# Three-layer graph block: each engine's order within a turn rewritten, the layer boundary made chunk by chunk, tables loaded in three parts

## The chip, the cores and the metric

The kernel runs on one core of one Trainium2 chip. The metric is device time in microseconds (us) of one execution; the median of three runs of the kernel before is 1787.18 us. The engines: PE (TensorE, matmuls and transposes), DVE (VectorE), ACT (ScalarE), POOL (GpSimd, which here issues the indirect DMAs and multiplies one tile), SP (SyncE, which issues the plain DMAs).

## The reference

10,000 nodes with 512 features, 5,000 edges sorted by destination. First a three-layer graph network with batch norm:

```
x_l: h = x @ W[l].T ; agg = segment_sum(h[src] * norm, dst) + b[l]      (every node also has a loop edge)
     x = relu(gamma[l] * (agg - mean) * rsqrt(var + 1e-5) + beta[l])     (mean, var over all nodes)
```

`x` plus its result goes through a layer norm. Then an equivariant message layer over the same edges and another layer norm give the output. The change touches the three layers alone.

## The kernel before

Four stages follow each other: `order_edges` sorts edges and loads tables; `graph_layers` computes the three layers; `finish_gcn` adds and norms; `messages` and `touched` do the rest. All the edits but the first (the table loads at the end of `order_edges`) are in `graph_layers`.

Nodes are held in 20 blocks of four tiles a layer, features on the partitions, in four chunks `c` of 128 features. `kinds` names the blocks P P E P E P ... E P E E: an E (edge) block has 4 x 127 nodes that are destinations of edges, a P (plain) block 4 x 123 nodes that are not. In an E block the sums over the edges are made first ("merge") and added to the block's own rows ("join").

Each engine's program is a list of turns t; in turn t block t is multiplied and the blocks ahead are prepared. There is no planner: the order is written out by hand in each engine's `body(layer, t)`, and semaphores order the engines. In a turn, j counts the four output chunks or the four tiles of a block:

- PE: `products(t, j)`, 12 matmuls of 492 or 508 columns (high and low parts of both factors, three products for each of four chunks; each first waits for `lo` of its chunk); `back(t-1, j)`, four transposes that give node rows for the next layer's table (layers 0 and 1 only); `turn_in(t+2, j)`, four transposes of gathered rows (layer 0 only); `merge(t+2, j)`, four matmuls with the edge table (E blocks).
- ACT: `copy` of a product out of PSUM into `aggT` (L891), `high` (L844, L846), `relu` of the block loaded from `z` (L860), `sources`, relu of gathered rows (L867), `rows_out` copies of `back` (L899), `plain` (L853).
- DVE: `low` (L757, L759), `bn_stats` of a copied chunk (L796), merge with the running carry (L737, L739), `join` (L750), `shifts` of gathered rows (L768), `build` of the edge tables (layer 0).
- POOL: indirect DMAs: `own` (L646: node rows into R, layer 0), `gather` (L631: edge source rows), `place` (L636: node ids of E blocks), `leave` (L652: result rows into the next layer's table), the scatter of payload (L676, layer 1); and in layers 1 and 2 one multiply of an E block by its own weights (L670).
- SP: loads of `z`, stores of `aggT` to `z`, stores of R (L608).

Rings: R has 8 buffers, G 4 (8 with R's first four in layers 1 and 2), X 3, yhi, ylo, aggT and every PSUM tile 2, V 4. In layer 0 the ids of E block b are fetched in turn b-5 and used in turn b-3.

At a layer's end turn NB does the last `back`s, `rows_out` copies and scatters. Then DVE makes the batch-norm factors of all four chunks at once (`factors`, L702 to L710) and ACT the root (L916), which stands behind the last `rows_out` copy in ACT's order; only then does ACT take relu and high of the next layer's first blocks.

## Time and profile before

| | us |
|---|---|
| median of three runs | 1787.18 (1779.79 to 1788.62) |
| the profiled execution | 1788.72 |
| its span | 1786.9 |
| PE busy | 1383.3 (77%) |
| DVE busy | 1219.7 (68%) |
| POOL busy | 965.3 (54%) |
| ACT busy | 946.7 (53%) |
| granted clock of PE, mean | 0.868 of full speed |

The stages in time: ordering to 170 us; layer 0's products from 200.5 to 536, layer 1's from 554.5 to 855, layer 2's from 868 to 1181; the rest to 1787. Busy shares are averages over stages with different limits, so what a stage is bound by is read from its own windows and waits. Busy time of a matmul counts its whole passage, so neighbours overlap: what a matmul costs in a row of them is the distance from one start to the next.

### The profile page before, as it was taken

What the parts mean: (1) busy time and instruction counts of PE and PEld (TensorE: products, weight loads), DVE (VectorE), ACT (ScalarE), POOL (GpSimd) and SP (SyncE); (2) the same over time, 40 slices, a digit from 0 to 9 for tenths busy, and PEclk for the clock granted to TensorE, in tenths of its full rate; (3) what the DMA queues carried; (4) which work ended last, traced back from release to release, by engine and by line L of the source; (5) the groups of instructions that cost most, each with busy time, mean ns of one, the idle gap of its engine ahead of it and who ended that gap; (6) DMA issues with size and microseconds to landing.
All of it is one profiled execution on the core that took longest, in us unless ns stands there. A gap on an engine that the chain in (4) does not pass through costs nothing. (4 is left out here: it accounts for less than half of the span.)

```text
span 1786.9 us, 27336 instructions
## 1 busy us (share of the span) xinstructions
PE 1383.3 (77%) x8020; PEld 1181.3 (66%) x8020; DVE 1219.7 (68%) x3372; ACT 946.7 (53%) x1900; POOL 965.3 (54%) x966
## 2 busy tenths in 40 slices
PE   4574699999995999999698988863555269999733
PEld 3454588888784888888576777753444158888622
DVE  6357467666565676767577768857777459999765
ACT  3471244353335767674555554436778624444476
POOL 4770777777744677777523223204777744343146
PEclk8797799999998999999899999976655679999955
DMA  2002878888775677776644545359999433333112
GB/s 60 2 2 82 263 244 282 274 274 272 261 266 198 216 258 239 252 253 208 219 135 157 171 161 168 113 196 298 412 401 404 201 101 85 92 89 87 42 69 111
DMA packets 130634, 340.36 MB, mean 190 GB/s; under 512 B 34940, under 2 KB 67188, under 8 KB 127702
## 3 DMA queue, kind: packets, MB, share of 16 engines
q1 hardware_dynamic: 74198, 175.45, 28.0%
q0 software_dynamic: 56320, 163.51, 27.4%
q8 instruction: 55, 0.90, 0.2%
q14 instruction: 61, 0.50, 0.1%
HBM read 166.40 MB, written 177.40 MB: 192 GB/s over the span
## 5 line engine op out<-in xcount | busy, mean ns | idle before, releaser
L946 PE MATMUL ps_b<-yhi,whi 128*128 128x492 f32 (+1 forms) x960 | 399.4, 416 | 33.9 <-DVE ylo L759 25.2
L946 PE MATMUL ps_b<-ylo,whi 128*128 128x492 f32 (+1 forms) x960 | 380.2, 396 | 0.0
L946 PE MATMUL ps_b<-yhi,wlo 128*128 128x492 f32 (+1 forms) x960 | 379.9, 396 | 0.0
L891 ACT COPY aggT<-ps_b 128x492 f32<-128x492 f32 (+1 forms) x240 | 137.4, 573 | 307.1 <-PE ps_b L946 306.8
L796 DVE BATCH_NORM_STATS2 stat<-aggT 128x6 f32<-128x492 f32 (+1 forms) x240 | 162.3, 677 | 155.4 <-ACT aggT L891 155.4
L652 POOL DMA_INDIRECT rows<-rows_out,node_at x160 | 175.1, 1095 | 123.7 <-ACT rows_out L899 84.6
L946 PEld LDWEIGHTS ps_b<-yhi,whi 128*128 128x128 f32 x960 | 186.9, 195 | 67.5 <-issue 26.2
L946 PEld LDWEIGHTS ps_b<-yhi,wlo 128*128 128x128 f32 x960 | 185.1, 193 | 38.5
L946 PEld LDWEIGHTS ps_b<-ylo,whi 128*128 128x128 f32 x960 | 186.4, 194 | 30.4 <-issue 0.5
L759 DVE SCALAR_TENSOR_TENSOR ylo<-X,bn_scale,yhi 128x492 fp32r<-128x492 f32 (+1 forms) x160 | 147.3, 962 | 78.0 <-ACT yhi L846 78.0
L670 POOL TENSOR_TENSOR X<-X,own_row 128x2032 f32<-128x2032 f32 x20 | 91.6, 4579 | 176.1 <-ACT X L860 176.0
L1173 PE MATMUL fin_ps_x<-ident,fin_X 128*123 128x128 f32 (+1 forms) x320 | 72.1, 396 | 99.1 <-DVE fin_xr L1098 73.0
L1173 PEld LDWEIGHTS fin_ps_x<-ident,fin_X 128*123 128x123 f32 (+1 forms) x320 | 63.9, 292 | 115.0 <-DVE fin_xr L1098 77.4
L737 DVE SCALAR_TENSOR_TENSOR V<-cont,carry,ps_m 128x127 f32<-128x127 bf16 x480 | 132.4, 339 | 3.6 <-PE ps_m L933 2.3
L646 POOL DMA_INDIRECT R<-in_x,node_at x80 | 93.4, 1167 | 71.1 <-DVE rows_out L813 47.0
L1047 POOL DMA_INDIRECT x<-fin_x,node_at x80 | 78.8, 985 | 94.7 <-ACT fin_x L1150 74.6
L846 ACT ACTIVATE yhi<-X,bn_scale 128x492 fp32r<-128x492 f32 (+1 forms) x160 | 104.9, 705 | 23.3 <-DVE X L750 23.2
L899 ACT COPY rows_out<-ps_c 123x512 f32<-123x512 f32 (+1 forms) x160 | 94.6, 592 | 33.8 <-DMA rows<-rows_out,node_at 32.4
L933 PE MATMUL ps_m<-sel,G 128*128 128x128 f32 x640 | 89.8, 286 | 23.0 <-DVE carry L739 14.4
L957 PEld LDWEIGHTS ps_c<-ident,aggT 128*127 128x127 f32 (+1 forms) x640 | 94.0, 187 | 14.1 <-ACT aggT L891 0.8
L860 ACT ACTIVATE X<-X,bn_shift 128x492 f32<-128x492 f32 (+1 forms) x160 | 100.4, 702 | 1.6 <-DVE bn_scale L708 1.6
L933 PEld LDWEIGHTS ps_m<-sel,G 128*128 128x128 f32 x640 | 81.6, 199 | 29.2 <-issue 17.0
(346 smaller groups left out, 3196.5 us busy)
## 6 DMA issues: line engine op xcount, KB each, us to landing
z<-aggT SPq DMA_DIRECT2D x30, 1016.0 KB, 4.8
z<-aggT SPq DMA_DIRECT2D x30, 984.0 KB, 6.0
x_rows<-R SPq DMA_DIRECT2D x80, 256.0 KB, 4.3
fin_xr<-x_rows SPq DMA_DIRECT2D x20, 1024.0 KB, 8.3
X<-z SPq DMA_DIRECT2D x20, 1016.0 KB, 7.5
X<-z SPq DMA_DIRECT2D x20, 984.0 KB, 7.6
fin_X<-z SPq DMA_DIRECT2D x10, 1016.0 KB, 12.5
fin_X<-z SPq DMA_DIRECT2D x10, 984.0 KB, 13.5
```

Of the source, the lines that this page charges most:

```text
L652: pool.indirect_dma_start(table[layer], bass.IndirectOffsetOnAxis(ap=k.node_at[:, i:i + 1], axis=0), f.rows[j][:], None, bounds_check=m.N ...
L737: nc.vector.scalar_tensor_tensor(V3[i % 4][:, c, :], k.cont[:, i, 0:EPT], f.carry[i % 2][:, c:c + 1], ps[:, c, 0:EPT], ALU.mult, ALU.add)
L759: nc.vector.scalar_tensor_tensor(f.ylo[g % 2][:, c, 0:n], y, s.scale[:, c:c + 1], hi, ALU.mult, ALU.subtract).then_inc(x["lo"], 1)
L796: nc.vector.bn_stats(k.stat[:, j, 6 * t:6 * t + 6], f.aggT[t % 2][:, j, 0:n]).then_inc(x["counted"], 1)
L846: nc.scalar.activation(f.yhi[g % 2][:, c, 0:n], f.X[g % 3][:, c, 0:n], ACT.Copy, scale=s.scale[:, c:c + 1]).then_inc(x["hi"], 1)
L860: nc.scalar.activation(f.X[g % 3][:, c, 0:n], f.X[g % 3][:, c, 0:n], ACT.Relu, bias=s.shift[:, c:c + 1]).then_inc(x["act_x"], 1)
L891: nc.scalar.copy(f.aggT[t % 2][:, j, 0:cols(t)], f.ps_b[j % 2][:, 0:cols(t)]).then_inc(x["copied"], 1)
L899: nc.scalar.copy(f.rows[j][0:n, :], f.ps_c[j % 2][0:n, :]).then_inc(x["rows"], 1)
L933: o = nc.tensor.matmul(f.ps_m[i % 2][:, c * P:(c + 1) * P], buffer[:, c * P:(c + 1) * P], k.sel[:, i * P:(i + 1) * P], start=True, stop=True)
L946: o = nc.tensor.matmul(f.ps_b[j % 2][:, 0:n], w[:, c, j * P:(j + 1) * P], y[g % 2][:, c, 0:n], start=(c == 0 and i == 0), stop=(c == C - 1 ...
L957: o = nc.tensor.transpose(f.ps_c[j % 2][0:n, c * P:(c + 1) * P], f.aggT[b % 2][:, c, col:col + n], k.ident[:])
L1173: o = nc.tensor.transpose(k.ps_x[j % 2][0:n, c * P:(c + 1) * P], f.X[b % 3][:, c, col:col + n], k.ident[:])
```

## The change

In words, by engine:

- `order_edges` loads only the first of now three parts of the match and own tables (tiles 0 to 4; before 0 to 7 and 8 to 39, both here). SP loads parts 1 (5 to 16) and 2 (17 to 39) in turns -1 and 0 of layer 0.
- POOL: the first gathers each wait for the memset of their own buffer, not for all twelve; ids of E block b are fetched in turn b-4; the multiply is made in two halves of two chunks; the payload scatters go four to each plain turn; turn NB is gone, its scatters come after the last turn.
- DVE: `join` works by chunk over all four tiles of a block and not by tile over all four chunks; lows of a plain block all come at the top of the turn; `shift` is spread over j; the first E block of layers 1 and 2 is merged and joined in turn 1.
- ACT: highs of a plain block at the top of the turn, two relus before and two after copy 0; `source` spread over j; its own order for turn 0 of layers 1 and 2.
- The boundary: in the last turn of a layer each chunk's aggregate, root and factors follow its statistics, and relu, high and low of that chunk of the next layer's block 0 follow at once; the last block's `back`s and `rows_out` copies stand partly before and partly behind the next layer's first product.

```diff
@@ order_edges, SP
-            for i, (lo, hi) in enumerate(k.parts):
-                sp.dma_start(k.sel[...], a.match_rows[...]...).then_inc(k.match_in[i], 16)
-                sp.dma_start(own[...], a.own_rows[...]...).then_inc(k.own_in[i], 16)
+            lo, hi = k.parts[0]
+            sp.dma_start(k.sel[...], a.match_rows[...]...).then_inc(k.match_in[0], 16)
+            sp.dma_start(own[...], a.own_rows[...]...).then_inc(k.own_in[0], 16)
@@ graph_layers
     def each_turn(body, layer):
-        for t in range(-5, NB + 1):
+        for t in range(-5, NB):
             body(layer, t)
+    def ends(layer, t):
+        return t == NB - 1 and layer < L - 1
@@ SP, after the four R stores of a turn
+                if layer == 0 and 0 <= t + 1 < len(k.parts) - 1:
+                    tables(t + 2)
@@ POOL
             def own(b, j):
...
+                if n < 8:
+                    pool.wait_ge(x["zero"], n + 1)
...
+            def weigh(layer, b, h):
+                g, o = layer * NB + b, m.nth(b)
+                pool.wait_ge(x["act_x"], C * (g - NB) + 2 * h + 2)
+                view = f.X[g % 3][:, 2 * h:2 * h + 2, 0:4 * EPT]
+                nc.gpsimd.tensor_tensor(view, view, k.own_row[...]..., ALU.mult).then_inc(x["weighted"], 1)
...
-                    if layer == 0 and m.edges(t + 5):
-                        place(t + 5, j)
+                    if layer == 0 and m.edges(t + 4):
+                        place(t + 4, j)
                     if layer < L - 1 and runs(t - 1):
                         leave(layer, t - 1, j)
-                    if layer > 0 and j == 2 and m.edges(t + 2):
...
+                    if layer > 0 and j in (1, 2) and m.edges(t + 2):
+                        weigh(layer, t + 2, j - 1)
-                    if layer == 1 and j >= 2 and runs(t):
+                    if layer == 1 and m.plain(t):
...
-            pool.wait_ge(x["zero"], 12)
             for layer in range(L):
                 each_turn(body, layer)
                 if layer < L - 1:
+                    for j in range(4):
+                        leave(layer, NB - 1, j)
                     for r in range(4):
                         pool.wait_ge(put[r], 16 * NB * (layer + 1))
@@ DVE
-            def moments(layer, c):
-            def factors(layer):
+            def factors(layer, c):
+                col, one = slice((layer - 1) * C + c, (layer - 1) * C + c + 1), slice(c, c + 1)
+                dve.wait_ge(x["counted"], C * (layer * NB - 1) + c + 1)
                 nc.vector.bn_aggr(s.mv[:, c, :], k.stat[:, c, :]).then_inc(x["var"], 1)
+                dve.wait_ge(x["var"], C * (layer - 1) + c + 1)
+                v.link(nc.vector.tensor_tensor(s.mean[:, one], s.mv[:, c, 0:1], k.bsg[:, col], ALU.add))
+                v.link(nc.vector.tensor_tensor(s.mean[:, one], k.bsg[:, col], s.mean[:, one], ALU.subtract))
+                dve.wait_ge(x["root"], C * (layer - 1) + c + 1)
+                ge(dve, x["act_x"], C * (layer - 1) * NB)
+                nc.vector.scalar_tensor_tensor(s.shift[:, one], ...).then_inc(x["factor"], 1)
+                v.link(nc.vector.reciprocal(s.scale[:, one], s.std[:, one]))
+                nc.vector.tensor_tensor(s.scale[:, one], ...).then_inc(x["factor"], 1)
...
+            def join(layer, b, c):
+                view = f.X[g % 3][:, c, 0:4 * EPT].rearrange("p (e n) -> p e n", e=4)
+                dve.wait_ge(x["carried"], layer * ET + 4 * o + 4)
...
+                nc.vector.tensor_tensor(view, view, f.V[:, :, c, :], ALU.add).then_inc(x["joined"], 1)
...
             def body(layer, t):
+                late = layer > 0 and t == 1
+                if layer > 0 and t == 0:
+                    (diag and the reset of carry, as before at the layer's start)
+                if late:
+                    for j in range(4):
+                        shift(layer, 2, j)
+                elif m.edges(t + 1):
+                    for c in range(C):
+                        join(layer, t + 1, c)
+                if m.plain(t + 1) and t >= (0 if layer > 0 else -1):
+                    for c in range(C):
+                        low(layer, t + 1, c)
                 for j in range(4):
                     if layer == 0 and m.edges(t + 2):
+                        weighted_x(t + 2, j)
+                    if m.edges(t + 1) and j in (1, 2) and not late:
+                        low(layer, t + 1, 2 * j - 2)
+                        low(layer, t + 1, 2 * j - 1)
+                    if layer > 0 and m.edges(t + 3) and t >= 0:
+                        shift(layer, t + 3, j)
                     if runs(t):
                         (bn_stats of chunk j)
+                    if ends(layer, t):
+                        factors(layer + 1, j)
+                        if j > 0:
+                            low(layer + 1, 0, j - 1)
+                    if m.edges(t + 2) and not (layer > 0 and t == 0):
+                        merge(layer, t + 2, j)
+                    if late and j in (1, 2):
+                        merge(layer, 2, 2 * j - 2)
+                        merge(layer, 2, 2 * j - 1)
+                    if late and j == 2:
+                        (all joins, then all lows, of block 2)
+                if ends(layer, t):
+                    low(layer + 1, 0, C - 1)
@@ ACT
+            def turn_0(layer):
+                for j in range(4):
+                    if j == 0:
+                        rows(layer - 1, NB - 1, 0)
+                        rows(layer - 1, NB - 1, 1)
+                    else:
+                        for c in ((), (0, 1), (2, 3), ())[j]:
+                            relu(layer, 1, c)
+                            high(layer, 1, c)
+                    copy(layer, 0, j)
+                    if j == 0:
+                        rows(layer - 1, NB - 1, 2)
+                        rows(layer - 1, NB - 1, 3)
+                    if j == 1:
+                        (trow from ps_m)
+                    if j == 2:
+                        relu(layer, 2, 0)
+                        relu(layer, 2, 1)
+                relu(layer, 2, 2)
+                relu(layer, 2, 3)
             def body(layer, t):
...
+                if m.plain(t + 1):
+                    for c in range(C):
+                        high(layer, t + 1, c)
                 if layer > 0 and runs(t + 2):
+                    for c in (0, 1) if m.plain(t + 1) else range(C):
+                        relu(layer, t + 2, c)
+                if late:
+                    for j in range(4):
+                        source(layer, 2, j)
                 for j in range(4):
+                    if runs(t):
+                        copy(layer, t, j)
+                    if ends(layer, t):
+                        act.wait_ge(x["var"], C * layer + j + 1)
+                        nc.scalar.activation(s.std[:, j:j + 1], s.mv[:, j, 1:2], ACT.Sqrt, ...).then_inc(x["root"], 1)
                     if layer == 0 and m.plain(t + 2):
                         plain(t + 2, j)
                     if layer < L - 1 and runs(t - 1):
+                        rows(layer, t - 1, j)
+                    if ends(layer, t):
+                        relu(layer + 1, 0, j)
+                        high(layer + 1, 0, j)
+                    if j == 0 and layer > 0 and runs(t + 2) and m.plain(t + 1):
+                        relu(layer, t + 2, 2)
+                        relu(layer, t + 2, 3)
+                    if m.edges(t + 1):
+                        for c in ((), (), (), range(C))[j] if late else (range(0, 2), range(2, 4), (), ())[j]:
+                            high(layer, t + 1, c)
+                    if layer > 0 and m.edges(t + 3):
+                        source(layer, t + 3, j)
@@ PE
                     if layer > 0 and t == 0 and j == 0:
+                        back(layer - 1, NB - 1, 2)
+                        back(layer - 1, NB - 1, 3)
                         (the matmul that spreads diag into ps_m)
...
-                if t == 0:
-                    for j in range(4):
-                        merge(layer, j)
+                if ends(layer, t):
+                    back(layer, t, 0)
+                    back(layer, t, 1)
@@ build
-        k.parts = ((0, 8), (8, ET))
+        k.parts = ((0, 5), (5, 17), (17, ET))
-                f.V = [m.sb(f"V{i}", [P, C * m.EPT]) for i in range(4)]
+                f.V = m.sb("V", [P, 4, C, m.EPT])
```

## Rows read from the trace of the kernel before

**Rows 1.** Windows: stretch, length, busy us (instructions) by engine, granted clock, DMA share, GB/s.
```profile
200.00:505.00 305.00, 295.79 (x1708) 259.78 (x1707) 194.62 (x458) 126.86 (x242) 234.91 (x210) 0.98 0.81 268
...
550.00:560.00 10.00, 5.53 (x13) 4.49 (x14) 4.03 (x6) 9.14 (x16) 6.73 (x7) 0.50 0.54 163
...
605.20:854.90 249.70, 247.74 (x1361) 214.93 (x1360) 172.81 (x372) 167.54 (x299) 186.33 (x141) 0.99 0.71 242
...
923.00:1181.60 258.60, 228.97 (x1075) 190.06 (x1073) 192.87 (x365) 132.16 (x224) 64.78 (x33) 0.95 0.45 149
```
**Rows 2.** Waits of PE, 165 to 1200 us: us in total, times, longest.
```profile
PE ps_x L967 <- DMA R<-in_x,node_at: 30.9, 11, 18.9
PE ps_m L933 <- DVE carry L739: 27.0, 15, 3.0
PE ps_b L946 <- DVE ylo L759: 25.2, 2, 15.0
```
**Rows 3.** Timeline of PE: the first product of six turns (start, us).
```profile
664.56 0.48 PE L946 MATMUL ps_b<-yhi,whi 128*128 128x492 f32 x1
...
677.04 0.48 PE L946 MATMUL ps_b<-yhi,whi 128*128 128x508 f32 x1
...
693.56 0.47 PE L946 MATMUL ps_b<-yhi,whi 128*128 128x492 f32 x1
...
986.04 0.47 PE L946 MATMUL ps_b<-yhi,whi 128*128 128x492 f32 x1
...
996.81 0.39 PE L946 MATMUL ps_b<-yhi,whi 128*128 128x508 f32 x1
...
1018.72 0.47 PE L946 MATMUL ps_b<-yhi,whi 128*128 128x492 f32 x1
```
**Rows 4.** Timeline of the start: start, us, engine, idle before.
```profile
171.64 4.27 DVE L813 MEMSET R<- 128x512 f32 x8 [2.90 <-PEq L100]
...
178.98 1.05 POOL L646 DMA_INDIRECT R<-in_x,node_at  x1 [47.02 <-DVE rows_out L813]
...
200.47 0.76 PE L946 MATMUL ps_b<-yhi,whi 128*128 128x492 f32 x1
```
**Rows 5.** DMA issues, 200 to 500 us: median us from issue to landing.
```profile
R<-in_x,node_at POOLq DMA_INDIRECT x70, 4.7
...
node_at<-others,free_row POOLq DMA_INDIRECT x35, 3.6
```
**Rows 6.** Timeline of PE: first products two turns apart, layer 0.
```profile
252.37 0.47 PE L946 MATMUL ps_b<-yhi,whi 128*128 128x492 f32 x1
...
284.65 0.47 PE L946 MATMUL ps_b<-yhi,whi 128*128 128x492 f32 x1
```
**Rows 7.** Timeline of the boundary of layers 0 and 1.
```profile
535.80 0.40 PE L946 MATMUL ps_b<-yhi,wlo 128*128 128x508 f32 x1
...
546.44 0.58 ACT L899 COPY rows_out<-ps_c 127x512 f32<-127x512 f32 x1 [6.86 <-DMA rows<-rows_out,node_at]
...
554.48 0.75 PE L946 MATMUL ps_b<-yhi,whi 128*128 128x492 f32 x1 [15.03 <-DVE ylo L759]
```
**Rows 8.** Groups by line, whole span: busy us, mean ns, idle before and releaser.
```profile
L796 DVE BATCH_NORM_STATS2 stat<-aggT 128x6 f32<-128x492 f32 (+1 forms) x240 | 162.3, 677 | 155.4 <-ACT aggT L891 155.4
...
L846 ACT ACTIVATE yhi<-X,bn_scale 128x492 fp32r<-128x492 f32 (+1 forms) x160 | 104.9, 705 | 23.3 <-DVE X L750 23.2
...
L697 DVE BATCH_NORM_AGGREGATE bn_mv<-stat 128x2 f32<-128x120 f32 x8 | 5.6, 697 | 0.3
```
**Rows 9.** Timeline of layer 2: DVE's lows and POOL's multiply.
```profile
1003.87 4.55 POOL L670 TENSOR_TENSOR X<-X,own_row 128x2032 f32<-128x2032 f32 x1 [20.61 <-ACT X L860]
...
1004.42 5.17 DVE L759 SCALAR_TENSOR_TENSOR ylo<-X,bn_scale,yhi 128x492 fp32r<-128x492 f32 x2 [3.73 <-ACT yhi L846]
```
**Rows 10.** Timeline of layer 1: DVE's merge beside POOL's multiply.
```profile
604.45 4.59 POOL L670 TENSOR_TENSOR X<-X,own_row 128x2032 f32<-128x2032 f32 x1
...
605.47 1.12 DVE L737 SCALAR_TENSOR_TENSOR V<-cont,carry,ps_m 128x127 f32<-128x127 bf16 x4
```

More of the change, by code:

```diff
@@ L625, in _, with gather @@
         def _(pool):
-            def gather(layer, i, source):
+            def gather(layer, b, j):
+                i = 4 * m.nth(b) + j
                 buffer, sem, _ = ring_g(layer, i)
@@ L863, in sources @@
-            def sources(layer, b):
-                for i in range(4 * m.nth(b), 4 * m.nth(b) + 4):
-                    act.wait_ge(x["shifted"], (layer - 1) * ET + i + 1)
-                    buffer = ring_g(layer, i)[0]
-                    nc.scalar.activation(buffer[:], buffer[:], ACT.Relu).then_inc(x["relued"], 1)
+                if b == 0:
+                    act.wait_ge(x["factor"], 2 * C * (layer - 1) + 2 * c + 1)
+                nc.scalar.activation(f.X[g % 3][:, c, 0:n], f.X[g % 3][:, c, 0:n], ACT.Relu,
+                                     bias=s.shift[:, c:c + 1]).then_inc(x["act_x"], 1)
@@ new lines, in source, with copy @@
+            def source(layer, b, j):
+                i = 4 * m.nth(b) + j
+                act.wait_ge(x["shifted"], (layer - 1) * ET + i + 1)
+                buffer = ring_g(layer, i)[0]
+                nc.scalar.activation(buffer[:], buffer[:], ACT.Relu).then_inc(x["relued"], 1)
+            def copy(layer, t, j):
+                g = layer * NB + t
+                act.wait_ge(x["product"], C * g + j + 1)
+                if j == 0:
+                    ge(act, x["back"], 4 * (min(g, (L - 1) * NB + 1) - 1))
+                    ge(act, x["counted"], C * (g - 1))
+                    ge(act, kept[t % 2], 16 * (g // 2))
+                nc.scalar.copy(f.aggT[t % 2][:, j, 0:cols(t)], f.ps_b[j % 2][:, 0:cols(t)]).then_inc(x["copied"], 1)
@@ L895, in body @@
-                    if layer < L - 1 and runs(t - 1):
-                        n = m.tile(t - 1, j)[1]
-                        act.wait_ge(x["back"], 4 * (g - 1) + j + 1)
-                        ge(act, put[j], 16 * (g - 1))
-                        nc.scalar.copy(f.rows[j][0:n, :], f.ps_c[j % 2][0:n, :]).then_inc(x["rows"], 1)
-                if layer > 0 and t == 0:
-                    sources(layer, 2)
+                    if layer < L - 1 and runs(t - 1):
+                        rows(layer, t - 1, j)
@@ L970, in body @@
             def body(layer, t):
+                late = layer > 0 and t == 1
                 for j in range(4):
@@ L982, in body @@
                         turn_in(t + 2, j)
-                    if m.edges(t + 2) and t > 0:
-                        merge(layer, 4 * m.nth(t + 2) + j)
-                if t == 0:
-                    for j in range(4):
-                        merge(layer, j)
+                    if m.edges(t + 2) and not (layer > 0 and t == 0):
+                        merge(layer, t + 2, j)
+                    if late and j in (1, 2):
+                        merge(layer, 2, 2 * j - 2)
+                        merge(layer, 2, 2 * j - 1)
+                if ends(layer, t):
+                    back(layer, t, 0)
+                    back(layer, t, 1)
                 if layer == 1 and 0 <= t - 3 < C:
```

201 lines of the change are left out of this document (82 added, 119 removed).

## The prediction
> **What bounds the kernel now.** I read the table of windows, then the waits of TensorE (PE), then the timelines round the places where it idles. The change lives in the graph stage, from about 170 to 1182 us. There PE is busy 296 of 305 us in layer 0, 247.7 of 249.7 in the later part of layer 1, and only 229 of 258.6 in layer 2 [rows 1]. PE's waits [rows 2] say what is missing: 30.9 us for gathered rows (18.9 of it in one wait at the start), 25.2 in two waits for DVE's low parts, at the layer boundaries, and 27.0 for DVE's carry, nearly all in layer 2. So PE is the bound except at four places, and the change touches all four.
>
> A turn's length is read from the first product of a turn to the next. Layer 1: 664.56, 677.04, 693.56, so 12.5 us for a turn without merges and 16.5 with. Layer 2: 986.04, 996.81, 1018.72, so 10.8 and 21.9 [rows 3]. Layer 2 has no `back` (12.5 - 10.8 = 1.7 us a turn), so its merge turn should take 16.5 - 1.7 = 14.8 at PE's own speed; it takes 20.7 to 21.9.
>
> **1. The start, -9.** The first product starts at 200.47, right behind the last transposed tile of block 1. POOL's first gather (178.98) waited for all twelve memsets, though a gather into R0 needs one: the eight begin at 171.64, 0.53 us each, so POOL may start at 172.3, 6.7 earlier [rows 4]. The ids of block 2 are now fetched a turn later, so ahead of block 1's last tile stand 10 issues and not 11 or more; at 1.31 us each (1.01 + 0.30) it is issued at 172.3 + 13.1 = 185.4, where now it is 178.98 + 11 x 1.31 = 193.4. Landing 4.7 us (median, [rows 5]; most of the broadcast tables no longer stand in front of it) gives 190.1, the product 191: -9.5. The two later table parts move 4.6 MB into turns -1 and 0; the transfers there have no PE wait that I can name, so I take 0.5 for them. If they delay one gather each, it is some 3 us.
>
> One edge speaks against this. Eleven more memsets now run beside POOL's first gathers. In layer 0 single POOL issues take 3.0 us where the usual one takes 1.03, so something can hold it; if all wait until the memsets end at 178.1, the gain is 3, not 9. The Trainium skill, "SBUF — State Buffer", section "SBUF: two separate sides", has a mechanism for it: a VectorE instruction in a two-port mode locks GpSimd out of writing descriptors. No row here shows memset and gather together.
>
> **2. Layer 0's rate, +1.** The two turns 252.37 to 284.65 take PE 32.3 us [rows 6]. POOL issues 210 transfers in the window of 305 us [rows 1] and idles for another engine only once, 6.5 us; so (305 - 6.5) / 210 = 1.42 us each, and 24 of them per two turns are 34.1 us. POOL is the slower one, and its lag grows by 1.8 us per two turns: that is why PE's stalls come from 335 on. The change issues the same 24, as 12 + 12 and not 16 + 8; worked at PE's pace, a tile is late only from a lag of some 12 us, where today 7 do: -4.5. Against it: the ids of an edge block are now fetched in the turn right before they are used. The last fetch is followed by one scatter, then by the gather that waits for it: 2 x 1.42 = 2.8 us after its issue, while it lands after 3.6 (median, [rows 5]). So POOL waits 0.8 to 1 us for each of 9 edge blocks, and with the wait before block 2 (3 us, inside term 1) this is +8 of POOL's time, of which PE sees about +5.5. Bounds: landings of 2.8 to 7.1 us give a wait of 0 to 4.3 a block.
>
> **3. Boundary 0 to 1, -11.** Last product 535.80; the next starts at 554.48 after 15.0 of idle [rows 7] and runs at the lower of PE's two levels (granted clock 0.50, [rows 1]), 0.41 apart instead of 0.22 to 0.23, for some 5 us. The chain between: copy, statistics, aggregate, then ACT waits 6.86 us for the scatter of four rows_out tiles before it comes to the root; then eight relus, four highs. Call E the last product's end (536.0). After the change ACT does per chunk: copy, a wait for statistics and aggregate (0.68 and 0.70, [rows 8]), root, rows, relu, high (0.705, overlapping by a tenth) = 0.5 + 1.5 + 0.4 + 0.55 + 0.65 + 0.6 = 4.2 us, against PE's 3.2. Over three chunks it falls 2.9 behind; the last copy is at E + 2.9, the last high ends 4.3 later (E + 7.2), the last low at E + 7.9. PE meanwhile does two `back`s (from E + 3.5) and the first six matmuls, then waits for chunks 2 and 3: product 0 done at E + 8.9. Today that is 559.5, E + 23.5. Then PE does the spread and products 1 to 3, held once by ACT (eight relu and high between its copies): turn 1 at E + 18.4 (now E + 40).
>
> Part of this is given back. The last rows_out tiles are copied only after the next layer's product 0, so the scatters end at E + 15.5 and block 2's gathers are issued at E + 15.5 to 19.4 (now E + 15.4 to 19.5), landing to E + 24. Turn 1, no longer turn 0's end, merges block 2. DVE queues shift(2) ahead of the statistics and ACT queues source(2) ahead of copy 0, so product 2 waits for the copy until E + 26; then the four merges, joins and lows of block 2 (9 us of DVE) end near E + 40 with PE idle for about 3 us. Turn 3 starts at E + 58, now at 605.2, E + 69: -11.
>
> **4. Rest of layer 1, -3.** Turn 3 to the last product, 249.5 us [rows 1]; by 12.5 and 16.5 [rows 3] it is seven turns of 12.5, turn 17 with merges 16.3, seven of 16.5, two of 12.8, in all 245. The difference is mostly one slow turn near the end. New order: ACT has 36 instructions of 0.6 us in a pair of 29, POOL 16 issues and the 4.6 multiply, 26 us of 29. Both fit, so 246.
>
> **5. Boundary 1 to 2, -13.5.** The same chain without `back`: turn 3 at E + 54.5. Now it is 923.0 with E = 854.8 [rows 1], so E + 68.
>
> **6. Rest of layer 2, -40.** Two turns take 32.7 [rows 3]. Why: ACT does four sources, four relus and two highs before copy 0. POOL's multiply of 4.55 us starts as relu ends, and a pair of DVE lows beside it takes 5.17 us [rows 9] where the next pair takes 1.36 (3.8 lost); the carry is then late, and PE waits 3 us and more for it. What now hides what: at a merge turn's start (0) ACT ends source 3 at 1.2, the four highs at 3.8, two relus at 5.1, copy 0 at 5.6, and PE wants it for product 2 at 7.4. DVE's four lows end at 4.7, before the multiply halves (5.1 to 7.4, 8.7 to 11). Beside them DVE then has statistics and merges, and in [rows 10] the four instructions of a merge take 1.12 us beside the multiply, as they do (1.10) without it. Merge 3 ends at 16.3, joins 18.7, lows of the edge block 23.9, and PE needs them at 25.6. The Trainium skill (same page and section) calls the port pair an exclusive lock that also binds a VectorE instruction with two SBUF inputs; by that, the low pair's 5.17 is such a lock, the trace agrees, and the joins and shifts are what must keep clear of it.
>
> So 14.8 + 10.8 = 25.6 a pair. From turn 3 to the last product, now 258: seven turns of 10.8, seven of 14.8, turn 17 with merges 14.6, two of 11 = 75.6 + 103.6 + 14.6 + 22 = 216. I add 2 for the tail: -40.
>
> **Sum.** -9 + 1 - 11 - 3 - 13.5 - 40 = -75.5, of the profiled execution's 1788.72 (span 1786.9): 1713. Its time is 1.5 above the median of the runs shown (1787.18), which run from 1779.79 to 1788.62, so 1713 stands. Less than 0.5% (9 us) can't be told from no change.
>
> **The rivals.**
> - A. Layer 2 stays bound by the exchange between ACT and DVE: half of the 7 us per pair is left. For: DVE is busy 24 of 32.7 us, and the edge lows end only 1.7 us before PE wants them. Against: the port loss of 3.8 goes. 8 x 3.5 = 28: 1741.
> - B. Layer 0 gets slower: each id fetch lands at the longest seen, 7.1: 9 x 4.3 = 39, less the 5.5 counted: 1713 + 33 = 1746. For: DMA engines are busy 81% there. Against: the median of 3.6.
> - C. The memsets hold the first gathers until 178.1 (term 1's other end): +6, 1719.
> - D. Even turns take layer 0's stalls away altogether: all 14 us over 32.3 a pair: 1713 - 13 = 1700.
> - E. Slower than before: the clock. Four short waits a turn in place of one long one leave PE at the lower of its two levels (0.41 against 0.23 a matmul). Each matmul there costs 0.18 us; layer 2 has 960. From 420 of them (76 us) nothing is gained, from 470 it is slower; at 600, 1713 + 108 = 1821. Against: today's layer 2, with longer waits, has 0.95 of full clock, layer 1 has 0.99 [rows 1].
> - F. The early first block isn't early: ACT now orders four roots between relus and copies, eight changes of function a boundary. At 1.5 us each they would eat both boundary gains: 1713 + 24 = 1737. Against: in the finish stage roots of 0.28 us stand between other activations with no gap.
>
> **How the numbers follow.** Forecast (1713 +-9) 0.57, A 0.14, B 0.08, C 0.07, D 0.08, E 0.03, F 0.03. The main case alone is 1704 to 1722. To leave no more than 2 in 10 outside, the range takes in C, D and most of A: 1694 to 1743. Slower by over 0.5%: E, 0.03. Within: 0.02, for sums of A, B and F. Faster: 0.95.
>
> **What would show it.** First product near 191; POOL's gather at 172. Layer 0's last product about 528. PE idle at a boundary under 6 us in all, and the first product of layers 1 and 2 within 6 us of the last before. Layer 2's merge turns at 14.8, none of DVE's low pairs over 1.5. POOL halves of 2.3. Waits for carry under 3 us in all. Wrong if layer 0 keeps its end near 536 (term 2), if the merge turns stay over 18 (term 6), or if turn 3 of layer 1 comes later than 62 us behind layer 0's last product (term 3).

## The result, and the profile after

The changed kernel takes 1742.76 us (median of 4 runs, 1735.61 to 1745.04) against 1787.9 before: ratio 0.9751, 95% interval [0.9711, 0.9791]. The forecast was 1713, its range 1694 to 1743 just holds the median (the profiled execution, 1743.42, lies just outside), and the gain is 45 us where 75.5 were expected. The page of the kernel after, engine by engine:

```profile
span 1741.7 us, 27484 instructions
PE 1375.5 (79%) x8020; PEld 1179.2 (68%) x8020; DVE 1205.7 (69%) x3400; ACT 948.3 (54%) x1906; POOL 975.6 (56%) x986
```

Its windows, for the stretches of [rows 1] (columns as there; layer 0, then turn 3 of layers 1 and 2 to their ends):

```profile
200.00:505.00 305.00, 286.71 (x1640) 249.96 (x1639) 185.75 (x438) 122.80 (x229) 229.91 (x202) 0.98 0.80 268
613.60:858.80 245.20, 245.20 (x1361) 213.25 (x1360) 182.35 (x383) 168.61 (x304) 184.71 (x146) 1.00 0.72 248
922.70:1136.60 213.90, 213.31 (x1075) 181.66 (x1073) 169.85 (x365) 132.10 (x224) 64.27 (x43) 1.00 0.53 184
```

In layers 1 and 2 PE is now busy the whole stretch, at full clock: the same 1075 matmuls of layer 2 take 213.9 us and not 258.6. In layer 0 it is busy 286.7 of 305 where it had been 295.8, and POOL got through 202 instructions and not 210. Each stage, measured from the starts of PE's products in the two profiled executions:

| stage | before | after | predicted | found |
|---|---|---|---|---|
| ordering, up to the first memset | 171.6 | 176.4 | 0 | +4.8 |
| first memset to first product | 28.8 | 19.8 | -9 | -9.0 |
| layer 0, first to last product | 335.3 | 351.5 | +1 | +16.2 |
| boundary 0 to 1, up to turn 3 | 69.4 | 65.9 | -11 | -3.5 |
| rest of layer 1 | 249.3 | 244.8 | -3 | -4.5 |
| boundary 1 to 2, up to turn 3 | 68.5 | 64.3 | -13.5 | -4.2 |
| rest of layer 2 | 258.0 | 213.4 | -40 | -44.6 |
| after the layers | 605.9 | 605.6 | 0 | -0.3 |

The ordering stage has the same work in both; in the experiments below, those on another chip apart, its end lies between 170.6 and 177 with no pattern, so I take the +4.8 for scatter and not for an effect of the change. The same scatter, up to 6 us, can stand in every time below, so an edit's worth is read from its own stage. Two terms carry the error: layer 0 (15 us) and the two boundaries (17). PE's waits, 165 to 1200 us, against [rows 2]:

```profile
PE ps_x L1041 <- DMA R<-in_x,node_at: 31.5, 15, 9.2
...
PE ps_b L1020 <- ACT aggT L912: 14.3, 2, 7.2
...
PE ps_c L1031 <- ACT aggT L912: 6.1, 2, 3.2
PE ps_b L1020 <- DVE ylo L782: 4.6, 2, 2.4
```

The 27 us for DVE's carry are gone, the 25.2 for the low parts are 4.6. New are two waits of 7 us for ACT's copy, one in turn 1 of each of layers 1 and 2. And the waits for rows in layer 0 are as long as before, although the first of them, 18.9, is down to 9.2: the rest grew from 12 to 22. Behind these stands POOL. Its waits, 165 to 505 us:

```profile
POOL R L666 <- DVE R L856: 47.2, 3, 46.6
POOL R L666 <- DMA node_at<-others,free_row: 19.6, 10, 7.6
```

and the longest of them in POOL's timeline:

```profile
217.09 1.01 POOL L654 DMA_INDIRECT node_at<-others,free_row  x1 [0.30 <-issue]
225.75 1.00 POOL L666 DMA_INDIRECT R<-in_x,node_at  x1 [7.65 <-DMA node_at<-others,free_row]
```

For blocks 2 and 4 the last fetch of the ids is the issue right before the gather that uses them, for the others one scatter stands between. POOL works in order and stands still until the ids have landed. It happens for every edge block: 3.1 us for block 2, 7.65 for block 4 (its fetch stands behind 2.9 MB of tables), 0.75 to 1.5 for the others.

### The profile page after: what moved, and what is told of

Read it like the earlier page. It is cut to its first block and busy times, and to the rows that moved or that the text cites. A ratio compares the mean times of both kernels' runs of the same rounds, so it can differ in the third digit from the quotient of the medians.

```text
span 1741.7 us, 27484 instructions
## 1 busy us (share of the span) xinstructions
PE 1375.5 (79%) x8020; PEld 1179.2 (68%) x8020; DVE 1205.7 (69%) x3400; ACT 948.3 (54%) x1906; POOL 975.6 (56%) x986
## 5 line engine op out<-in xcount | busy, mean ns | idle before, releaser
L1020 PE MATMUL ps_b<-yhi,whi 128*128 128x492 f32 (+1 forms) x960 | 397.1, 414 | 18.9 <-ACT aggT L912 14.3
L672 POOL DMA_INDIRECT rows<-rows_out,node_at x160 | 180.8, 1130 | 110.4 <-ACT rows_out L918 63.3
L679 POOL TENSOR_TENSOR X<-X,own_row 128x1016 f32<-128x1016 f32 x40 | 96.4, 2412 | 131.5 <-ACT X L896 131.3
L782 DVE SCALAR_TENSOR_TENSOR ylo<-X,bn_scale,yhi 128x492 fp32r<-128x492 f32 (+1 forms) x160 | 111.8, 745 | 29.3 <-ACT yhi L881 28.9
L1031 PE MATMUL ps_c<-ident,aggT 128*127 128x128 f32 (+1 forms) x640 | 97.9, 276 | 8.6 <-ACT aggT L912 6.1
L896 ACT ACTIVATE X<-X,bn_shift 128x492 f32<-128x492 f32 (+1 forms) x160 | 103.9, 708 | 0.2 <-DVE bn_scale L733 0.2
L254 POOL DMA_INDIRECT others<-ord_nodeid,ord_place_node x80 | 78.4, 979 | 38.9 <-issue 23.5
```

Of the source, the lines that this page charges most:

```text
L672: pool.indirect_dma_start(table[layer], bass.IndirectOffsetOnAxis(ap=k.node_at[:, i:i + 1], axis=0), f.rows[j][:], None, bounds_check=m.N ...
L679: nc.gpsimd.tensor_tensor(view, view, k.own_row[:, 4 * o:4 * o + 4, :].rearrange("p t n -> p (t n)") .unsqueeze(1).to_broadcast([P, 2, 4 * ...
L782: nc.vector.scalar_tensor_tensor(f.ylo[g % 2][:, c, 0:n], y, s.scale[:, c:c + 1], hi, ALU.mult, ALU.subtract).then_inc(x["lo"], 1)
L896: nc.scalar.activation(f.X[g % 3][:, c, 0:n], f.X[g % 3][:, c, 0:n], ACT.Relu, bias=s.shift[:, c:c + 1]).then_inc(x["act_x"], 1)
L1020: o = nc.tensor.matmul(f.ps_b[j % 2][:, 0:n], w[:, c, j * P:(j + 1) * P], y[g % 2][:, c, 0:n], start=(c == 0 and i == 0), stop=(c == C - 1 ...
L1031: o = nc.tensor.transpose(f.ps_c[j % 2][0:n, c * P:(c + 1) * P], f.aggT[b % 2][:, c, col:col + n], k.ident[:])
```

## Experiments: layer 0

```diff
  e1_ids5
-                    if layer == 0 and m.edges(t + 4):
-                        place(t + 4, j)
+                    if layer == 0 and m.edges(t + 5):
+                        place(t + 5, j)
```


> The changed kernel with one thing undone: the ids of an edge block are fetched five turns ahead again, not four (16 and 8 issues a pair of turns in place of 12 and 12). Theory 1 (the id fetch one turn before its use makes POOL, which sets layer 0's pace, wait): POOL's waits for node_at, 19.6 us in the changed kernel, fall under 4; layer 0 from first to last product goes from 351.5 back towards 335; whole time about 1743 - 15 = 1728. Theory 2 (the two table parts now moved into the layer slow it): layer 0 keeps 347 or more, the time stays within 5 us of 1743. Theory 3 (the order 12 and 12 itself is worse for PE): like theory 1 here, and told from it by the next kernel.

Measured 1730.76 us, ratio to before 0.9675 [0.9651, 0.97] (the change: 0.9751). Layer 0 takes 336.1.

```diff
  e2_ids6 (in place of the two lines above)
+                    ids = {-2: 2, -1: 4, 14: NB - 1}.get(t, t + 6 if 0 <= t < 13 else -1)
+                    if layer == 0 and m.edges(ids):
+                        place(ids, j)
```


> The changed kernel with the ids of edge blocks 4 to 18 fetched in turn b-6 (4: turn -1; 19: turn 14), so 12 and 12 issues a pair stay and no fetch is used in the next turn. Theory 1 (the wait): node_at waits vanish but for block 2; layer 0 at 335 or below, time 1725 to 1728. Theory 3 (the order 12 and 12): layer 0 stays at 345 to 351, time 1740. Theory 2 (tables): no change, 1743.

Measured 1724.19, ratio 0.9638 [0.9613, 0.9663]; layer 0 takes 338.8. Of POOL's 19.6 us of waits for ids this line of its waits is left:

```profile
POOL R L666 <- DMA node_at<-others,free_row: 2.6, 1, 2.6
```

Nothing but the distance between fetch and use was changed. By the medians 19 us went, but that this is what POOL had waited is luck: in the profiled executions 5.7 of them are the ordering stage, which the edit doesn't touch, and layer 0 is 12.7 shorter. All runs together give a better price. In the eight on chips with the usual ordering stage and with the change's ids and tables (the change, e5, e6, e7, e9, e13b, e14b, e15b), layer 0 takes 349.4 to 354.7 us and POOL waits 19.6 to 23.3 for ids; in the four with early ids (e1, e2, e4, e16b) layer 0 takes 334.2 to 338.8 and POOL waits 0.3 to 2.8. So some 19 us of waits cost layer 0 some 16. The 12 and 12 order did no harm.

```diff
  e3_tab4 (e4_ids6_tab4: this and the ids of e2)
-                if layer == 0 and 0 <= t + 1 < len(k.parts) - 1:
-                    tables(t + 2)
+                if layer == 0 and t in (-1, 4):
+                    tables(1 if t < 0 else 2)
```


> The changed kernel with the last table part (tiles 17 to 39) loaded in turn 4 and not in turn 0; ids as in the change. Theory 1: only the one long id wait behind these tables (7.65 us) goes, the eight short ones (1.1 each) stay; layer 0 shrinks by 4 to 8, time 1737. Theory 2 (tables, 2.9 MB in front of gathers): layer 0 falls by 12 to 16, time 1729.

> Both: ids in turn b-6 and the last table part in turn 4. Theory 1: as with the ids alone, at most 3 better, since with the ids early no POOL wait stands behind the tables: 1725. Theory 2: as with the tables alone. If the two causes add (id waits and the delay of gathers behind the tables): layer 0 at 330, time 1722.

Measured 1745.7, ratio 0.9743 [0.9708, 0.9778], and 1725.01, 0.9643 [0.9618, 0.9667]. Moved alone, the tables give nothing: layer 0 takes 361.6 in the profiled execution, 10 us more than in the change, and POOL waits 23.9 us for ids, only 4 more; the other 6 stay unexplained. The wait for block 4 falls to 2.2 us, but that for block 8, right behind the moved tables, grows to 6.3, and that for block 6, with no tables near it, to 4.2. So how long a fetch takes varies from one to the next, and both my theories promised a gain for this run that did not come. With the ids early it matters little where the tables stand (1724.19 and 1725.01; layer 0 338.8 and 334.2).

```diff
  e8_zero12
-                if n < 8:
-                    pool.wait_ge(x["zero"], n + 1)
...
+            pool.wait_ge(x["zero"], 12)
```


> The changed kernel with POOL waiting for all twelve memsets again before its first gather; the ids of block 2 still come late. Theory 1 (the wait for the memsets held the start): the first gather starts about 6.5 us behind the first memset (172.3 and 178.98 in terms of before), and the first product 26 us behind it, where the change has 19.9 and before 28.8; so 6 of the 9 us of the start are this wait, the rest the ids. Theory 2 (the ids alone): the first product stays 20 to 21 us behind the first memset.

This kernel and the next ones called e10, e11 and e12 ran on a chip where the kernel before took 2008 us: in all four the ordering stage ends near 274 us and not 172. Layer 0 (371 to 382 us) and all that follows the layers (664 to 677) are longer there too, so of these four I use only the start and layers 1 and 2, whose steady turns agree with the other chips to 0.1 us; e12, with the change's layer 2, has its 213.4 there. The medians can be compared only with before on the same chip. e8 has one execution, 1934.38. From first memset (274.18) to first product (299.8) e8 needs 25.6 us; the three others, with the change's waits, 19.6 to 20.1. So 5.8 of the 9 us of term 1 are the wait for all memsets. With the ids early again (e1) the distance is 22.6, 2.8 more than the change has: that is the other part.

## Experiments: layer 2

```diff
  e6_whole
-                pool.wait_ge(x["act_x"], C * (g - NB) + 2 * h + 2)
-                view = f.X[g % 3][:, 2 * h:2 * h + 2, 0:4 * EPT]
+                if h == 0: return
+                pool.wait_ge(x["act_x"], C * (g - NB) + C)
+                view = f.X[g % 3][:, :, 0:4 * EPT]
...
  e7_srctop: ACT's four sources at the head of the merge turn, behind highs
  e9_lowsplit (same for low in DVE's body)
-                if m.plain(t + 1): (four highs)
+                if m.plain(t + 1) and not (layer > 0 and t > 1): (four highs)
...
+                    if layer > 0 and t > 1 and m.plain(t + 1) and j < 2:
+                        high(layer, t + 1, 2 * j); high(layer, t + 1, 2 * j + 1)
```


> The changed kernel with POOL's multiply of an edge block in one piece again, after all four relus. Theory 1 (layer 2 gained because DVE's lows no longer stand beside the multiply, whatever its size): the multiply starts after relu 3, some 9 us into the merge turn, DVE's lows end at 8, so merge turns stay at 14.4 to 15 and the time within 4 us of 1743. Theory 2 (the halves are what gained): DVE's shared-port work falls on the long multiply again, merge turns of 16 or more, 7 x 2 in layer 2: 1757 or more.

> The changed kernel with ACT's four sources (relu of gathered rows) in one piece in the merge turn, behind the highs and ahead of the relus, and not spread over the turn before. Theory 1 (what ACT does ahead of copy 0 set the merge turn): ahead of copy 0 stand 4 sources of 0.6 us more, copy 0 comes about 2 us after PE wants it, merge turns of layer 2 go from 14.4 to 16 to 17: 7 x 2 = 14, and less in layer 1: 1757 to 1765. Theory 2 (DVE's order and the port were the whole cost): merge turns stay under 15, time within 4 us of 1743.

> The changed kernel with highs (ACT) and lows (DVE) of a plain block of layers 1 and 2 in two pairs again, at j=0 and j=1 of the merge turn (from turn 2 on); the multiply stays in halves. Theory 1 (port: a pair of lows beside a multiply half is held until the half ends): the second pair of lows falls on a half of 2.4 us and takes about 3 to 3.8 us in place of 1.3, the merges behind it are late: merge turns of 15.5 to 17 in layer 2, time 1750 to 1760. Theory 2 (the halves leave gaps enough): no pair over 2 us, merge turns 14.4 to 15, time within 4 us of 1743.

Measured 1743.27 (ratio 0.9749 [0.9721, 0.9777]), 1753.68 (0.9803 [0.9778, 0.9828]) and 1743.14 (0.9743 [0.9719, 0.9767]). The whole multiply costs nothing in the steady merge turns (14.4), because the lows are over when it starts; the last turns of the layer make 3.6 us of it. The sources behind the highs give merge turns of 15.6 (PE has eight waits for a source, of up to 0.8), less than expected, and layer 2 is 7.1 us longer. And in e9 the lows do fall on the halves, DVE's and POOL's timelines:

```profile
1037.81 3.00 DVE L782 SCALAR_TENSOR_TENSOR ylo<-X,bn_scale,yhi 128x492 fp32r<-128x492 f32 x2 [1.67 <-ACT yhi L884]
...
1042.48 2.14 DVE L782 SCALAR_TENSOR_TENSOR ylo<-X,bn_scale,yhi 128x492 fp32r<-128x492 f32 x2
```
```profile
1037.26 2.37 POOL L679 TENSOR_TENSOR X<-X,own_row 128x1016 f32<-128x1016 f32 x1 [15.13 <-ACT X L899]
...
1041.05 2.38 POOL L679 TENSOR_TENSOR X<-X,own_row 128x1016 f32<-128x1016 f32 x1
```

A pair of lows takes 1.39 alone and 3.00 and 2.14 here; yet the merge turns but the last (15.4) stay at 14.4 to 14.5, for DVE has that much room, and layer 2 is 2.8 longer. The theory of the port as the cause by itself fell. So I put back more at a time:

```diff
  e10_oldact: e9, with four sources, then four relus, ahead of the highs
  e11_oldall: e10 and e6, and DVE:
-                    if layer > 0 and m.edges(t + 3) and t >= 0: shift(layer, t + 3, j)
+                    if layer > 0 and m.edges(t + 3) and 0 <= t < 2: shift(layer, t + 3, j)
+                if layer > 0 and t > 1 and m.edges(t + 3):      (behind j's loop)
+                    for j in range(4): shift(layer, t + 3, j)
  e14b_halves: e10 with these late shifts, multiply in halves
  e15b_spread: e10 with e6, shifts spread
```


> The changed kernel with ACT's order of the merge turns as before (four sources, four relus, then highs in two pairs, each ahead of a copy) and DVE's lows of the plain block in two pairs; DVE's shifts stay spread over the turn, joins go by chunk, the multiply stays in halves. Each of these alone was worth 0 (lows and highs in pairs) and 11 us (sources). Theory 1 (layer 2's gain is ACT's order ahead of copy 0, and it adds up): merge turns of layer 2 at 18 or more, time 1743 + 11 + 14 = 1768 or more. Theory 2 (DVE's shifts and the whole multiply make the rest): merge turns at 16, time 1755 to 1760.

> As the kernel named before, and also DVE's four shifts in one piece at the turn's end and POOL's multiply in one piece: all of the order of layers 1 and 2 before the change but the joins, the boundary and the payload scatters. Both theories expect layer 2's merge turns at 20 to 21.9 and layer 2 40 us longer than in the change, 1785. If it stays under 1770, the joins (by chunk over four tiles in place of by tile) are what gained.

> The changed kernel with ACT's order of the merge turns as before, lows in pairs, and DVE's four shifts in one piece at the end of the turn; the multiply stays in halves. Theory 1 (late shifts start a chain: shifts, sources, relus, highs, lows, statistics, merge, all one behind the other, and it is the chain's length that makes the turn; the multiply only adds 3.8 us where the lows fall on it): merge turns of 17 to 19 in layer 2, 20 to 30 us more than the change. Theory 2 (only the multiply in one piece hurts): merge turns at 14.4 to 15. Theory 3 (only the late shifts hurt): 20.8, as with all undone.

> The changed kernel with ACT's order of the merge turns as before, lows in pairs and the multiply in one piece; DVE's shifts stay spread over the turn. Theory 1: the lows fall on the long multiply (a pair of over 3.5 us), but the chain starts 2.5 us earlier, so merge turns of 15.5 to 18 in layer 2, 10 to 25 us more than the change. Theory 2 (only the multiply in one piece hurts): 20.8, as with all undone. Theory 3 (only the late shifts hurt): 14.4.

| | multiply | shifts | merge turn of layer 2 | turn 3 to the end | ratio to before |
|---|---|---|---|---|---|
| before | whole | late | 19.2 to 21.9 | 258.0 | 1 |
| e11 | whole | late | 19.2 to 21.9 | 258.3 | 0.9874 [0.9825, 0.9923] (other chip) |
| e15b | whole | spread | 17.6 to 19.8 | 241.8 | 0.9923 [0.9892, 0.9954] |
| e14b | halves | late | 16.0 (last 17.9) | 226.4 | 0.9822 [0.9794, 0.9851] |
| e10 | halves | spread | 14.4 (last 18.4) | 216.7 | 0.9697 [0.9642, 0.9752] (other chip) |
| the change | halves | spread | 14.4 | 213.4 | 0.9751 |

Neither theory of e10 held: ACT's old order and the lows in pairs are together worth 3 us of the layer (one turn of 18.4). The other three stand on top of this order, so the four kernels are a square: multiply halved or whole, shifts spread or late. Whole alone adds 25 us (e15b), late alone 10 (e14b), both together 42 (e11), which with the 3 is the whole loss. From DVE's and POOL's timelines of e15b:

```profile
1029.36 5.27 DVE L784 SCALAR_TENSOR_TENSOR ylo<-X,bn_scale,yhi 128x492 fp32r<-128x492 f32 x2 [4.45 <-ACT yhi L886]
1034.55 0.68 DVE L835 BATCH_NORM_STATS2 stat<-aggT 128x6 f32<-128x508 f32 x1
1035.15 1.10 DVE L762 SCALAR_TENSOR_TENSOR V<-cont,carry,ps_m 128x127 f32<-128x127 bf16 x4
```
```profile
1028.87 4.59 POOL L681 TENSOR_TENSOR X<-X,own_row 128x2032 f32<-128x2032 f32 x1 [18.18 <-ACT X L901]
```

and of e14b, DVE:

```profile
1042.36 2.48 DVE L789 TENSOR_TENSOR G<-G,trow 128x512 f32<-128x512 f32 x4
1048.57 1.76 DVE L782 SCALAR_TENSOR_TENSOR ylo<-X,bn_scale,yhi 128x492 fp32r<-128x492 f32 x2 [3.73 <-ACT yhi L887]
```

What PE waits for from turn 3 on, first in e15b, then in e14b:

```profile
PE ps_m L1016 <- DVE carry L764: 21.0, 7, 3.5
```
```profile
PE ps_b L1030 <- ACT aggT L918: 7.6, 7, 1.1
```

I read the merge turn as one chain: shifts, sources, relus, highs, lows, statistics, merge 0, and PE's matmuls of merge 2. In e15b its lows are held until the multiply ends, 3.9 us, and the turn grows by 3.2 to 4.8 (5.4 in the last). In e14b the chain starts with four shifts behind the last statistics, and the turn grows by 1.6. Both together cost 6.4. So neither theory's pure form holds; the multiply in one piece under the lows is the larger part (25 of 45 us), late shifts the smaller (10), and 7 come only with both. Lows that are over before a whole multiply starts (e6), or that meet only a half of it (e9), cost under 4 us. Lows under the whole multiply with the change's order of ACT was not run, so the 25 holds with ACT's old order.

## Experiments: the boundary

```diff
  e5_late (turn 1 of layers 1 and 2; the same on DVE with shift)
-                if late:
-                    for j in range(4): source(layer, 2, j)
                 for j in range(4):
                     if runs(t): copy(layer, t, j)
...
+                    if late:
+                        source(layer, 2 + j // 2 * 2, j % 2 * 2)
+                        source(layer, 2 + j // 2 * 2, j % 2 * 2 + 1)
  e12_loadwait: e5, and SP
+                    if layer > 0 and t == 1: (wait for gathered tile 3 of block 2)
  e13b_weighfirst: e5, and POOL's two halves of block 2 at the head of turn 0
```


> The changed kernel with turn 1 of layers 1 and 2 reordered on DVE and ACT: shift and source of block 2 come after the statistics and the copy of chunks 0 and 1 (two each), those of block 4 after chunks 2 and 3; nothing is queued ahead of copy 0 any more. Theory 1 (head-of-line wait: four gathered tiles, of which the last lands some 11 us into the turn, stand in the order ahead of copy 0, and PE waits 7 us for that copy): from the first product to that of turn 3, now 58.6 us in layer 1 and 57.4 in layer 2, falls to about 52 each; whole time 1743 - 11 = 1732. Theory 2 (the gathered rows are simply late, and whatever is put first, the merges of block 2 wait for them): less than 2 us a boundary, 1740 or more.

> The changed kernel with turn 1 of layers 1 and 2 in the new order (copy first, then two shifts and sources) and, new, SP's load of block 4 in turn 1 waiting until the fourth gathered tile of block 2 has landed. Theory 1 (the gathers land late because the load of 1016 KB and the store of z run beside them): the fourth tile lands in 6 to 7 us and not 10.7, turn 1 falls from 23.4 to 20.5 in both layers, time 1736.7 - 5 = 1732. Theory 2 (they are late because the last rows are copied out and scattered late): turn 1 stays at 23, time 1736.

> The changed kernel with turn 1 in the new order (copies first) and POOL's two multiply halves of block 2 ahead of the gathers of block 4 in turn 0. Theory 1 (port: the pair of shifts takes 3.27 us because a half runs beside it): the halves run before the shifts, the pair takes 1.3, and turn 1 falls from 23.4 to about 21.5 in both layers: 4 us off what the copies-first kernel has. Theory 2 (ACT's six relus and the arrival of the gathered rows set it): turn 1 stays at 23 or more.

The wait in the change, ACT's timeline in turn 1 of layer 2, and DVE's:

```profile
892.96 0.63 ACT L903 ACTIVATE G<-G 128x512 f32<-128x512 f32 x1 [4.07 <-DVE G L789]
893.50 0.55 ACT L912 COPY aggT<-ps_b 128x492 f32<-128x492 f32 x1
```
```profile
884.96 3.26 DVE L789 TENSOR_TENSOR G<-G,trow 128x512 f32<-128x512 f32 x1 [1.73 <-DMA G<-rows,srci]
892.23 0.69 DVE L789 TENSOR_TENSOR G<-G,trow 128x512 f32<-128x512 f32 x1 [4.01 <-DMA G<-rows,srci]
```

PE's product 2 needs the copy at 893.50, and product 0, begun at 879.7, was done near 882.4, some 11 us earlier; four sources stand ahead of the copy, the last behind a gather that landed 10.7 us after its issue. PE then runs product 2 at the lower of its two levels, its matmuls 0.41 us apart and not 0.22 (the window's columns as in [rows 1]):

```profile
894.10:899.10 5.00, 5.00 (x12) 4.14 (x13) 4.82 (x14) 1.57 (x3) 0.95 (x1) 0.50 0.42 121
```

That is 1.8 us more in each of the two turns. With the copies first (e5) turn 1 takes 23.5 and 23.3 and not 28.1 and 26.9, and from the first product to that of turn 3 it is 55.8 and 53.8 and not 58.7 and 57.4: 6.5 us. Measured 1736.74, ratio 0.971 [0.9687, 0.9734], so 7 us. That is less than theory 1 asked (52 and 52), for 1.6 us of layer 1 are given back in turn 2, and it may not be all the edit's. In the runs with the usual ordering stage that leave turns 0 and 1 alone (e15b with its longer turn 2 apart), the boundary 1 to 2 takes 60.8 to 64.6, so e5's 60.6 hardly stands out; the boundary 0 to 1 takes 65.2 to 67.6 in them, and e5's 63.0 does. Of DVE's five waits for a gather, 14.9 us, one of 1.1 is left.

Holding the load back (e12: 1933.64, 0.9614 [0.956, 0.9668] on the other chip) did make the gather land sooner: SP lets the load go when it has landed, 6.4 us after its issue in layer 1 (699.18 against 692.82) and 7.3 in layer 2, where e5 has 10.9 and 9.4. Yet turn 1 stays at 23.5 and 23.3: the load delays the gather, but with the copies first the gather no longer sets the turn. In both kernels a pair of shifts falls on a multiply half (3.27 us in e5, layer 2; 3.79 in e12, layer 1; 1.28 alone). e13b (1736.12, 0.9711 [0.968, 0.9741]; turn 1 23.9 and 22.8) was to take the halves out of their way and did not; they now fall on the first pair. DVE and POOL in turn 1 of layer 1:

```profile
569.79 3.18 DVE L792 TENSOR_TENSOR G<-G,trow 128x512 f32<-128x512 f32 x2
```
```profile
567.11 4.70 POOL L679 TENSOR_TENSOR X<-X,own_row 128x1016 f32<-128x1016 f32 x2
```

So what the shifts under the multiply cost in turn 1 no run tells, and what is left of the boundary's error in turns 1 and 2 stays open.

Last, all that helped:

```diff
  e16b_best: e2, e5, e13b, and in turn 1 of layers 1 and 2
+  ACT: relus of block 3 behind copy 2; highs of block 2 ahead of copy 3; sources of block 4 last
+  DVE: join(layer, 2, c) followed by low(layer, 2, c - 1); shifts of block 4 last
```


> All that helped: ids of edge blocks in turn b-6, copies first in turn 1 of layers 1 and 2, multiply halves of block 2 first, and in turn 1 also ACT's relus of block 3 behind copy 2, the sources and shifts of block 4 behind the rest, joins and lows of block 2 interleaved. From the turns: 19 us from the ids, 6 from copies first, 4 from the halves, 2 x 3.5 from the rest (relus 1.4, shifts 1.2, joins 1.3 a boundary, less a little): 36 us below the change, 2.0% (ratio to before 0.955). If PE's rate at the lower clock after its waits eats part of it: 0.958.

Measured 1717.94 (6 runs, 1715.88 to 1721.72), ratio 0.9613 [0.9591, 0.9635]: 25 us better than the change, where 36 were expected. By stages it is 14.0 from layer 0 (the ids), 8.2 from the two boundaries, and 3.7 of the ordering stage's scatter. The boundaries are 1.0 and 0.7 shorter than in e5, so the rest gave next to nothing: turn 1 falls to 20.8 and 21.2, but turn 2 takes 19.2 and 18.3 where e5 has 17.9 and 16.1. The first pair of shifts takes 4.49 and 4.47 here, still beside the halves.

## Why the prediction was right or wrong

- **Term 1, the start (-9): right**, -9.0 from memset to product. Rival C is out: beside the eight memsets of R (176.44 to 180.71) POOL's gathers issue at 177.83, 179.19 and 180.50, of 1.05, 1.01 and 1.00 us. The Trainium skill, "SBUF — State Buffer", section "SBUF: two separate sides", tells of a lock by VectorE instructions in a two-port mode; these rows show none, and whether a memset is such an instruction no run here shows.
- **Term 2, layer 0's rate (+1): a step that failed**, +16.2. My own sign of being wrong came: the layer ends at 547.8, and at 543 without the ordering stage's 4.8, where I had 528. I had the mechanism, "POOL waits 0.8 to 1 us for each of 9 edge blocks", and for eight blocks it measured 0.75 to 1.5. Three things were mis-sized. Block 4's fetch met the moved tables (7.65), the very transfers of which I had written that they have no wait that I can name: I looked for a wait of PE, and it was POOL's. So POOL waits 16.5 us behind block 2 where I had 8. I let PE see only two thirds of this, and it sees about four fifths: the runs with early ids have some 19 us less of waits and some 16 less of layer 0. And of the -4.5 for even turns nothing clear is seen: the four runs with early ids take 334.2 to 338.8, before 335.3. Rival B named the right place at twice the price (the longest fetch in the rows of before took 7.3, not 7.1); D is out.
- **Terms 3 and 5, the boundaries (-24.5): the other step that failed, in the turns behind the first product**, -7.7. Here too my sign of being wrong came: turn 3 of layer 1 starts 65.9 us behind layer 0's last product, and I had set 62. The early first block is as forecast: ACT's chain per chunk takes 4.1 to 4.4 us (4.2 predicted), its last high ends at E + 7.4 and E + 7.1 (7.2). Rival F is out: roots of 0.29 stand between its copies and relus with no gap. Two places were mis-sized, by layer 1 (E is 548.0 there). Turn 1 begins at E + 21.2 and not 18.4: PE's second `back` waits 1.1 for the rows_out copy behind ACT's chain, the first product starts only at E + 7.0, and turn 0 takes 14.3. And turns 1 and 2 take 44.4 where I had 39.6: "product 2 waits for the copy" was there, but with gathers landing by E + 24. They were issued at E + 18.6 to 22.4, 3 us later than forecast, and the last took 11.0 us to land, at E + 33.5; so PE stands 7.2 us and then runs 12 matmuls at the lower level, 1.8 more. e5 gives back 3 of the 4.8. In layer 2 the same wait is 7.1 and the landing 10.7.
- **Term 4 (-3): right**, -4.5; PE is busy 245.2 of 245.2.
- **Term 6, layer 2 (-40): right**, -44.6; turns of 14.4 and 10.8 (14.8 and 10.8 predicted). Of its reasons the lows held by the multiply were the larger one, as I took it, but the halves were not needed for it (e6), the late shifts, which I had not priced, are the second, and ACT's order with the pairs of lows was worth only 3 us. Rivals A and E are out (clock 1.00).

## What to carry to other kernels

When an engine issues in order and sets the pace, a fetch whose result it needs itself goes two turns ahead, not one or two issues ahead: here four fifths of its waits came back as time, and the longest wait stood behind a bulk load put into the same turn. Before a part of a reordering is called the cause, or called idle, put the parts back together: here single parts undone were worth 3 to 7 us of layer 2 (e6, e7, e9), and all together 45. Look in the trace whether an experiment did what it was built for: e13b moved the multiply from one pair of shifts onto another. And read an edit's worth from its stage: e2's gain took in nearly 6 us from a stage that its edit does not touch. In a turn that starts with late data, what needs no such data goes first.

## What the runs showed of the hardware

- A pair of DVE instructions with two inputs in SBUF beside POOL's multiply that already runs ends 1.16 to 1.19 us behind it, wherever in it the pair began: 5.27 us beside 4.59, 3.00 beside 2.37, 2.14 beside 2.38 (lows), 3.18 beside 4.70 (shifts), against 1.36 to 1.39 and 1.28 alone; [rows 9] has it too. A shift that began 0.37 us ahead of a half (884.96 and 885.33) was held as well, 3.26 us, though starts on POOL are rough. A merge, which reads PSUM, takes 1.12 beside a multiply [rows 10] and 1.10 without. The Trainium skill, "SBUF — State Buffer", section "SBUF: two separate sides", calls the shared pair an exclusive lock between a VectorE instruction with two SBUF inputs and a GpSimd one that reads SBUF, taken by the one that starts first; the held pairs agree, the shift at 884.96 does not fit the last part.
- The ids of 128 rows land 3.9 us after their issue in the median, with DMA engines busy 80%; behind the tables POOL could go on only 8.7 us after it (217.09 to 225.75). At a layer's boundary row gathers landed 3.4 to 11.0 us after their issue.
- The ordering stage ended at 171 to 177 us in all profiled executions but four and at 273 to 274 in those, on another chip, with the same code; layer 0 and the stages behind the layers were longer there too. The steady turns of layers 1 and 2 (16.4, 12.5, 14.4, 10.8) agreed to 0.1 us.
